# Issuing the first two gathers of a mixture-of-experts stage from the end of the routing block

## The chip, the cores and the metric

The kernel runs on one core of one Trainium2 chip. A core has five engines that run their own instruction streams and meet only through semaphores: TensorE (PE), VectorE (DVE), ScalarE (ACT), GpSimd (POOL) and SyncE (SP), which here only issues DMAs. Sixteen DMA engines carry the transfers of all of them. The metric is the device time of one execution in microseconds (us), lower being better. The kernel before takes 1161.29 us (median of three runs, 1160.04 to 1161.42).

## The reference

Two layers of a gated cross-attention network on x of 4 x 1024 tokens x 256. Layer 0 is attention over 77 context rows (16 heads), then a mixture of 8 experts with the two best experts a token; layer 1 is attention again, then a feed-forward layer with rounded weights. The change lies between the routing and the experts of layer 0:

```
x = x + tanh(g_xattn[0]) * L0_xattn(layernorm(x), ctx)
# experts of layer 0, on xt = layernorm(x), 4096 rows of 256
S = sigmoid(xt @ Wg)                    # Wg 256 x 8
G, I = top_k(S, 2)
h = gelu(einsum('nd,edf->enf', xt, W1) + b1)   # W1 8 x 256 x 1024
y = einsum('enf,efd->end', h, W2) + b2         # W2 8 x 1024 x 256
x = x + tanh(g_ffn[0]) * (sum over the two chosen experts of G * y)
x = x + tanh(g_xattn[1]) * L1_xattn(layernorm(x), ctx)
x = x + tanh(g_ffn[1]) * L1_ffn(layernorm(x))
```

## The kernel before, in words

The program is a row of blocks. At the end of each block (line 720 stands for the routing block's in the profile) every engine drains its own work and meets the others; GpSimd collects the four other engines' arrivals, then releases them, and each branches to its stream of the next block. SP's stores may still be under way at that moment: its own drain does not wait for them.

**The routing block** (`routing`, lines 697 to 1312) does two things at once. It normalises the 4096 rows, stores them to the HBM tensor `xn_dram`, forms the logits, and works out which token stands in which of 71 groups of 128 places (`C.token_of`, one column a group). It also folds the weights of the second attention ("folding"): for eight pairs of heads PE projects weights, ACT copies the products to `kst` and `vst`, and SP stores them to HBM (lines 853 and 859). The weights of the first pairs, `wkv`, arrive in a ring of two; the last pairs read `wkv_late`. The last work of each engine in this block is: PE the eighth `invert` (line 1041), DVE `tile_first` and `C.token_of` (lines 1311 and 1312), ACT the last copies to `vst` (line 1104), SP the last two stores of `vst` (line 859), GpSimd its eighth product of line 918.

**The experts block** (`experts`) works through 40 tiles: 31 of two groups (256 rows) and 9 of one. For a tile, GpSimd gathers the rows group by group with an indirect DMA (line 1491, 128 KB each) into `xg`, which has two slots; PE transposes them (line 1506, two transposes a group) to `ps_x`; ACT makes the bf16 high part `xhi` (line 1578), DVE the low part `xlo` (line 1625); PE multiplies with W1 (line 1527, 48 matmuls), ACT applies GELU (line 1590) and PE multiplies with W2 (lines 1540 and 1546). Before its first tile PE waits for the biases `b1_rows` (SP, line 1398), transposes them (line 1553), and waits for ACT's copy (line 1573); only then come the four transposes of tile 0. SP, behind `b1_rows`, waits for tile 0's two gathers (line 1455) and then loads `b2_all` (1 MB, line 1456) and the first two pieces of the next weights (line 1410).

GpSimd issues the gathers of tiles 0 and 1 one behind the other; that of tile j, from 2 on, waits until PE has transposed tile j-2. Names in the profile carry the part's prefix: `exp_xg` is `xg` of the experts, `moe_first_rows` and `all_token_of` are tensors that outlive a block.

## Time and profile before

| what | value |
|---|---|
| median of three runs | 1161.29 us (1160.04 to 1161.42) |
| the profiled execution's own time | 1163.3 us |
| its span in the trace | 1161.2 us |
| PE busy | 1057.4 us, 91% of the span |
| DVE, ACT, POOL busy | 916.9, 834.7, 539.4 us |
| share of PE in the chain that ended last | 57% |
| `L1491 POOL DMA_INDIRECT`, 71 gathers | 84.4 us busy, 1188 ns mean |
| mean granted clock of TensorE | 0.975 |

The span is what the trace covers; 2.1 us of the profiled execution lie outside it. A row of the timeline gives the start and the length in us, the engine (PEld is PE's weight load, an engine's name with q at its end is its queue, where DMAs, drains and semaphores stand), the line of the kernel, the operands, and in brackets how long the engine had been idle and what released it. The granted clock is 1.00 where TensorE has 2.4 GHz and 0.50 where it has 1.2 GHz. Most of the program is left as it is; the boundary between the two blocks lies at 336.4 us of the span.

### The profile page before, as it was taken

Reading aid. Unit: us, or ns where it says so; the run is one execution under the profiler, and the core shown is the slowest. Engines: PE = TensorE matmul, PEld = TensorE weight load, DVE = VectorE, ACT = ScalarE, POOL = GpSimd, SP = SyncE. Lnnn points to the kernel's source line nnn. Section 1 sums busy time; section 2 is a strip of 40 time slices with the busy share of each in tenths; the row PEclk is TensorE's granted clock in tenths of the full one; section 3 lists DMA queues with packets and bytes.
Section 4 is the critical chain, followed back from the end, with each engine's and each line's share of the span. In section 5 each row is a group of like instructions: output and inputs, shape, how many; then the busy total and the mean of one; then the engine's idle time right before and its main releaser. Section 6 shows DMA issues by size and latency. Waiting matters only on the chain.

```text
span 1161.2 us, 26321 instructions
## 1 busy us (share of the span) xinstructions
PE 1057.4 (91%) x8919; PEld 775.3 (67%) x8919; DVE 916.9 (79%) x1960; ACT 834.7 (72%) x2382; POOL 539.4 (46%) x515
## 2 busy tenths in 40 slices
PE   6888888868969999999999999589999999889898
PEld 5666666645537777777777777357777777645477
DVE  5999999957845687666666667479999999789798
ACT  4988889836656456556556667378888888569896
POOL 5888888732252122122122111178889887500140
PEclk9999999979989999999999999889999999989899
DMA  6443334349672343333333335345252423010034
GB/s 150 118 128 110 110 110 133 123 128 284 189 206 61 53 137 90 118 101 121 124 104 120 121 115 161 112 127 161 68 158 67 154 74 92 28 38 0 1 119 137
DMA packets 128814, 132.12 MB, mean 114 GB/s; under 512 B 24792, under 2 KB 112973, under 8 KB 128557
## 3 DMA queue, kind: packets, MB, share of 16 engines
q1 hardware_dynamic: 119901, 112.17, 32.0%
q0 software_dynamic: 6480, 17.70, 5.5%
q8 instruction: 73, 1.20, 0.4%
q10 hardware_dynamic: 2304, 0.59, 0.3%
q14 instruction: 56, 0.46, 0.1%
HBM read 82.78 MB, written 47.64 MB: 112 GB/s over the span
## 4 chain that ended last, share of the span: by engine, by line
PE 57%; DVE 4%; ACT 4%; issue 2%; DMA 1%; POOL 1%; DVEq 0%; SPq 0%; ACTq 0%; POOLq 0%
PE exp_ps_h L1527 15%; PE exp_ps_y L1540 9%; PE a_ps_o L1953 9%; PE a_ps_sc L1937 8%; PE f_ps_h L2264 5%; PE exp_ps_y L1546 5%; PE a_ps_p L1924 3%; ACT exp_h L1590 2%; DVE f_hlo L2395 2%; PE exp_ps_x L1506 1%; PE f_ps L2447 1%; PE f_ps L2443 1%; PE f_ps_x L2255 1%; DVE all_xn L2404 1%; PE a_ps_x L1911 1%
## 5 line engine op out<-in xcount | busy, mean ns | idle before, releaser
L1590 ACT ACTIVATE exp_h<-exp_ps_h,exp_b_now 128x256 f32<-128x256 f32 (+1 forms) x320 | 124.7, 440 | 142.4 <-PE exp_ps_h L1527 142.4
L1491 POOL DMA_INDIRECT exp_xg<-xn,all_token_of x71 | 84.4, 1188 | 304.0 <-PE exp_ps_x L1506 288.5
L1527 PE MATMUL exp_ps_h<-exp_xhi,exp_w_now 128*128 128x256 bf16 (+1 forms) x1280 | 196.4, 263 | 5.9 <-DVE exp_xlo L1625 5.9
L1986 ACT ACTIVATE a_z<-a_ps_sc,a_nmx 128x77 f32<-128x77 f32 x512 | 159.3, 367 | 35.6 <-DVE a_nmx L2088 35.6
L1527 PE MATMUL exp_ps_h<-exp_xlo,exp_w_now 128*128 128x256 bf16 (+1 forms) x640 | 161.4, 263 | 0.0
L1703 DVE TENSOR_TENSOR exp_hlo<-exp_h,exp_hhi 128x512 bf16<-128x512 f32 (+1 forms) x160 | 99.4, 632 | 70.4 <-ACT exp_hhi L1597 68.5
L1540 PE MATMUL exp_ps_y<-moe_w2s,exp_hhi 128*128 x568 | 134.2, 379 | 1.3 <-DVE exp_y L1722 1.3
L1527 PEld LDWEIGHTS exp_ps_h<-exp_xhi,exp_w_now 128*128 128x128 bf16 x1280 | 120.6, 99 | 20.7 <-issue 8.3
L1986 ACT ACTIVATION_READ_ACCUMULATOR a_z<-a_ps_sc,a_nmx 128x1 f32 x512 | 127.0, 248 | 0.0
L1953 PE MATMUL a_ps_o<-a_v_now,a_phi 128*128 128x256 bf16 (+1 forms) x640 | 106.6, 272 | 2.3 <-DVE a_plo L2077 2.3
L1937 PE MATMUL a_ps_sc<-a_k_now,a_xhi 128*128 128x462 bf16 (+1 forms) x384 | 98.6, 341 | 3.4 <-DMA a_k_now<-fold_klo 2.2
L1597 ACT ACTIVATE exp_hhi<-exp_h 128x512 bf16<-128x512 f32 (+1 forms) x160 | 93.1, 582 | 5.0
L1540 PEld LDWEIGHTS exp_ps_y<-moe_w2s,exp_hhi 128*128 128x128 bf16 x568 | 55.5, 98 | 52.8 <-issue 1.5
L1953 PE MATMUL a_ps_o<-a_v_now,a_plo 128*128 128x256 bf16 x320 | 87.2, 272 | 0.0
L483 PE MATMUL a_ps_vo<-a_pT,a_vblk 128*32 128x128 f32 (+1 forms) x1088 | 59.8, 279 | 27.6 <-ACT a_pT L549 20.5
L1860 POOL DMA_INDIRECT a_yg<-y_slots,all_slots x64 | 65.4, 1022 | 41.5 <-DMA y_slots<-exp_y 26.2
L379 POOL TENSOR_TENSOR a_z<-a_z,a_rsum 128x1232 f32<-128x1232 f32 x32 | 72.0, 2250 | 6.7 <-DVE a_rsum L631 6.7
L1880 POOL TENSOR_TENSOR a_z<-a_z,a_rsum 128x1232 f32<-128x1232 f32 x32 | 71.7, 2239 | 5.9 <-DVE a_rsum L2065 5.9
L1546 PE MATMUL exp_ps_y<-moe_w2s,exp_hlo 128*128 x568 | 73.6, 273 | 0.0
L1716 DVE TENSOR_TENSOR exp_yb<-exp_ps_y,exp_b_all 128x256 f32<-128x256 f32 x71 | 30.1, 424 | 54.3 <-PE exp_ps_y L1546 51.8
L1546 PEld LDWEIGHTS exp_ps_y<-moe_w2s,exp_hlo 128*128 128x128 bf16 x568 | 55.6, 98 | 21.6
L483 PEld LDWEIGHTS a_ps_vo<-a_pT,a_vblk 128*32 128x32 f32 (+1 forms) x1088 | 36.1, 109 | 50.5 <-issue 23.9
(279 smaller groups left out, 2735.5 us busy)
## 6 DMA issues: line engine op xcount, KB each, us to landing
a_stage<-in_L_ffn_W_dram SPq DMA_DIRECT2D x64, 256.0 KB, 3.2
y_slots<-exp_y SPq DMA_DIRECT2D x71, 128.0 KB, 1.7
fold_k<-route_kst SPq DMA_DIRECT2D x16, 308.0 KB, 4.5
fold_v<-route_vst SPq DMA_DIRECT2D x16, 308.0 KB
exp_job_in<-fold_k SPq DMA_DIRECT2D x14, 352.0 KB, 3.3
exp_job_in<-fold_v SPq DMA_DIRECT2D x14, 352.0 KB, 3.3
a_x<-in_x_dram SPq DMA_DIRECT2D x32, 128.0 KB, 2.3
x<-a_xo SPq DMA_DIRECT2D x32, 128.0 KB, 1.7
```

The source lines that it names most:

```text
L379: pool.tensor_tensor(zt, zt, rsum[:, v, :].unsqueeze(2).broadcast_to((P, HEADS, KEYS)), ALU.mult).then_inc(s["norm_done"], 1)
L483: mm = pe.matmul(ps_v[32 * j:32 * j + 32, g * P:(g + 1) * P], vblk[0:n, bv % 2, c, half, :], pT[0:n, c, :], start=(c == mine[0]), stop=(c ...
L1491: pool.indirect_dma_start(out=xg[:, v, u, :], out_offset=None, in_=xn_dram[:, :], in_offset=bass.IndirectOffsetOnAxis(ap=at.bitcast(U32), ...
L1527: mm = pe.matmul(hidden[:, i, f % 2, slots(j)], w1_now[:, v, k, hl, f * P:(f + 1) * P], xx[:, k, slots(j)], start=(q == 0), stop=(q == len ...
L1540: pe.matmul(ps_y[:, u, :], hhi[:, v, f, mine], w2s[:, bass.ds(e * FCH + f, 1), 0:2 * D].rearrange("p o f -> p (o f)"), start=(f == 0), sto ...
L1546: mm = pe.matmul(ps_y[:, u, 0:D], hlo[:, v, f, mine], w2s[:, bass.ds(e * FCH + f, 1), 0:D].rearrange("p o f -> p (o f)"), start=False, sto ...
L1590: ins = act.activation(h[:, f, slots(j)], hidden[:, i, f % 2, slots(j)], ACT.Gelu_apprx_tanh, bias=b1_now[:, v, f:f + 1])
L1597: act.activation(hhi[:, v, 2 * i:2 * i + 2, slots(j)], h[:, 2 * i:2 * i + 2, slots(j)], ACT.Copy).then_inc(s["hhi_done"], 1)
L1703: dve.tensor_tensor(hlo[:, v, 2 * i:2 * i + 2, slots(j)], h[:, 2 * i:2 * i + 2, slots(j)], hhi[:, v, 2 * i:2 * i + 2, slots(j)], ALU.subtr ...
L1937: mm = pe.matmul(ps_sc[:, j, 0:n], xx[:, u, k, :], k_now[:, b % 2, k, hl, h0 * KEYS:h1 * KEYS], start=(i == 0), stop=(i == len(parts) - 1))
L1953: mm = pe.matmul(ps_o[:, 0:D], pp[0:n, c, :], v_now[0:n, bv % 2, hl, c, :], start=(c == 0 and pp is phi and hl == 0), stop=last)
L1986: ins = act.activation(z[:, u, h * KEYS:(h + 1) * KEYS], ps_sc[:, j, (h - SB[j][0]) * KEYS:(h - SB[j][0] + 1) * KEYS], ACT.Exp, bias=nmx[: ...
```

## The change

GpSimd issues the two gathers of tile 0 at the end of its routing stream, after its last product. It waits there for the stored rows, for PE's last projection out of `wkv`, and for a new semaphore that DVE raises with `C.token_of`. The gathers of the experts block begin with tile 1. Their target can no longer be memory of the experts block alone: `first_rows` is allocated ahead of both blocks, with the size of `xg` (2 slots x 2 groups x 256 columns), and the folding's `wkv` is a view of it. DVE raises the new semaphore in place of its own, for which it waited once more behind `C.token_of`. SP's wait for tile 0's gathers, and its place, are unchanged.

```diff
--- before.py
+++ after.py
@@ -782,7 +782,7 @@
         ps_n = ps_x[:, 0, :].rearrange("p (a n) -> p a n", a=2)
         names = ("const_step", "wg_in", "stats_done", "mean_done", "veps_done", "rstd_done", "xn_done", "turned", "xT_done",
                  "wg_zero", "lT_done", "lT_copied", "logits_done", "filled", "emptied", "exp_done", "step", "both_done", "counted", "low_done", "high_done",
-                 "place_done", "tile_done", "inv_done", "late_in")
+                 "place_done", "tile_done", "inv_done", "late_in", "token_of_done")
         s = {n: m.sem(n) for n in names}
         xn_stored = [m.sem(f"xn_stored{i}") for i in range(2)]
         C.rows_stored, C.row_chunks = xn_stored, NCH // 2
@@ -920,6 +920,15 @@
 
             run_inversion(times_tile)
 
+            for stored_rows in C.rows_stored:
+                pool.wait_ge(stored_rows, 16 * C.row_chunks)
+            pool.wait_ge(filled, proj_at[RING_H - 1] + 3)
+            pool.wait_ge(s["token_of_done"], 1)
+            for u in range(SUB):
+                pool.indirect_dma_start(out=C.first_rows[:, 0, u, :], out_offset=None, in_=xn_dram[:, :],
+                                        in_offset=bass.IndirectOffsetOnAxis(ap=C.token_of[:, u:u + 1].bitcast(U32), axis=0)
+                                        ).then_inc(C.first_gathered[u], 16)
+
         @block.tensor
         def _(pe):
             def turn(i):
@@ -1309,7 +1318,7 @@
                     tile_experts()
             dve.wait_ge(s["inv_done"], NRI)
             link(dve.tensor_scalar(tile_first[:, :], ps_inv[:, NSUB:2 * NSUB], float(P), None, ALU.mult))
-            link(dve.tensor_tensor(C.token_of[:, :], ps_inv[:, 0:NSUB], tile_first[:, :], ALU.add))
+            dve.tensor_tensor(C.token_of[:, :], ps_inv[:, 0:NSUB], tile_first[:, :], ALU.add).then_inc(s["token_of_done"], 1)
 
 
 def experts(nc, C, xn_dram, y_dram, split, b1, b2, w_in, w_out, folded):
@@ -1342,7 +1351,7 @@
         hhi = m.sb("hhi", [P, 2, FCH, SLOT_T], BF16)
         hlo = m.sb("hlo", [P, 2, FCH, SLOT_T], BF16)
         w1_now = m.sb("w1_now", [P, 2, KD, 2, F], BF16)
-        xg = m.sb("xg", [P, 2, SUB, D])
+        xg = C.first_rows
         y = m.sb("y", [P, SUB, D])
         yb = m.sb("yb", [P, SUB, D])
         job_in = m.sb("job_in", [P, 2, WIN])
@@ -1361,7 +1370,7 @@
                  "xlo_done", "h_done", "gelu_done", "hhi_done", "hlo_done", "y_done", "y_low", "y_sum",
                  "w_turned", "job_high", "job_done", "w_step", "scale_out", "scale_in")
         s = {n: m.sem(n) for n in names}
-        gathered = [[m.sem(f"gathered{v}_{u}") for u in range(SUB)] for v in range(2)]
+        gathered = [C.first_gathered, [m.sem(f"gathered1_{u}") for u in range(SUB)]]
         stored = [m.sem(f"stored{u}") for u in range(SUB)]
         job_loaded = [m.sem(f"job_loaded{i}") for i in range(2)]
         job_stored = [m.sem(f"job_stored{i}") for i in range(2)]
@@ -1478,7 +1487,7 @@
         @block.gpsimd
         def _(pool):
             def step(j, v, n):
-                if not has(j):
+                if not has(j) or isinstance(j, int) and j == 0:
                     return
                 if has(j - 2):
                     pool.wait_ge(s["turned_x"], j - 1)
@@ -2488,15 +2497,19 @@
             w0 = {"wq": io["L0_xattn_Wq"], "bq": io["L0_xattn_bq"], "wk": io["L0_xattn_Wk"], "bk": io["L0_xattn_bk"],
                   "wv": io["L0_xattn_Wv"], "bv": io["L0_xattn_bv"], "wo": io["L0_xattn_Wo"], "bo": io["L0_xattn_bo"]}
             w1 = {"wq": io["L1_xattn_w_q"], "wkv": io["L1_xattn_w_kv"], "wo": io["L1_xattn_w_out"]}
+            C.first_rows = mm.sb("first_rows", [P, 2, SUB, D])
             with ExitStack() as front:
                 fm = Mem(nc, front, C.sems, "front")
-                ahead = {"wkv": fm.sb("wkv", [P, 2, 2, 2, P]), "wq": fm.sb("wq", [P, 2, KD, P]), "wo": fm.sb("wo", [P, 2, D]),
+                wkv_now = C.first_rows[:, :, :, :].rearrange("p v u d -> p (v u d)").rearrange(
+                    "p (g k o n) -> p g k o n", g=2, k=2, o=2)
+                ahead = {"wkv": wkv_now, "wq": fm.sb("wq", [P, 2, KD, P]), "wo": fm.sb("wo", [P, 2, D]),
                          "x": fm.sb("x", [P, AHEAD_ROWS, D])}
                 ctx_rows = ahead["x"][0:KEYS, :, :].rearrange("k r d -> k (r d)")[:, 0:B * DC].rearrange("k (b c) -> k b c", b=B)
                 with nc.Block() as C.block:
                     prologue(nc, io, C, ctx_rows)
                     attention(nc, C, x_dram, x1_dram, w0, 0, split, v_dram, ahead, w1, (io["g_xattn"], io["g_ffn"]))
                 clear_semaphores(nc, C)
+                C.first_gathered = [m.sem(f"first_gathered{u}") for u in range(SUB)]
                 routing(nc, C, x1_dram, xn_dram, io["L0_ffn_Wg"], w1, folded, ahead)
             C.block = ctx.enter_context(nc.Block())
             experts(nc, C, xn_dram, y_dram, split, io["L0_ffn_b1"], io["L0_ffn_b2"], io["L1_ffn_W_in"],
```

GpSimd's stream around the end of the routing block (line 720), as a difference; L918 is its last product, `xn` the stored rows in HBM:

```order
 L918 TENSOR_TENSOR route_high_tok<-route_high_hot,route_iota 128x8x71 x8
+L928 DMA moe_first_rows<-xn,all_token_of 128x256 x2
 L720 UNCONDITIONAL_BRANCH
-L1478 UNCONDITIONAL_BRANCH
-L1491 DMA exp_xg<-xn,all_token_of 128x256 x71
...
+L1487 UNCONDITIONAL_BRANCH
+L1500 DMA moe_first_rows<-xn,all_token_of 128x256 x69
```

Two of the 71 gathers moved in front of the branch; 69 stay behind it.

SP's stream at the same place, of the kernel before:

```order
L859 DMA fold_v<-route_vst 77x4x256 x2
L720 UNCONDITIONAL_BRANCH
L1396 UNCONDITIONAL_BRANCH
L1398 DMA exp_b_rows<-in_L_ffn_b_dram 64x128
L1456 DMA exp_b_all<-in_L_ffn_b_dram 128x2048
L1410 DMA exp_job_in<-in_L_ffn_W_in_dram 128x2x256 x3
```

And of the changed kernel:

```order
L859 DMA fold_v<-route_vst 77x4x256 x2
L720 UNCONDITIONAL_BRANCH
L1405 UNCONDITIONAL_BRANCH
L1407 DMA exp_b_rows<-in_L_ffn_b_dram 64x128
L1465 DMA exp_b_all<-in_L_ffn_b_dram 128x2048
L1419 DMA exp_job_in<-in_L_ffn_W_in_dram 128x2x256 x3
```

Nothing moved on SP but the line numbers: `b1_rows` is still issued behind the meeting of the engines, in the queue that carries the last stores of the folding.

## Rows read from the trace of the kernel before

**Rows 1.** Timeline, 318 to 350 us: start, length, engine, line, operands, idle before and releaser.

```profile
333.76 0.23 DVE L1312 TENSOR_TENSOR all_token_of<-route_ps_l,route_tile_first 128x71 int32<-128x71 f32 x1
...
335.29 0.77 SPq L859 DMA_DIRECT2D fold_v<-route_vst  x2
336.56 0.54 SPq L1398 DMA_DIRECT2D exp_b_rows<-in_L_ffn_b_dram  x1
337.41 1.23 POOL L1491 DMA_INDIRECT exp_xg<-xn,all_token_of  x1 [5.71 <-issue]
...
338.94 1.52 POOL L1491 DMA_INDIRECT exp_xg<-xn,all_token_of  x1 [0.30 <-issue]
...
339.65 0.37 PE L1553 MATMUL exp_ps_y<-all_ident,exp_b_rows 64*128 64x64 f32 x1 [6.19 <-DMA exp_b_rows<-in_L_ffn_b_dram]
340.06 0.22 ACT L1573 ACTIVATE exp_b1T<-exp_ps_y 128x64 f32<-128x64 f32 x1 [4.31 <-PE exp_ps_y L1553]
...
340.57 0.66 PE L1506 MATMUL exp_ps_x<-all_ident,exp_xg 128*128 128x128 f32 x2 [0.55 <-DMA exp_xg<-xn,all_token_of]
340.77 0.95 POOL L1491 DMA_INDIRECT exp_xg<-xn,all_token_of  x1 [0.30 <-issue]
...
342.29 0.69 PE L1506 MATMUL exp_ps_x<-all_ident,exp_xg 128*128 128x128 f32 x2 [1.07 <-DMA exp_xg<-xn,all_token_of]
...
344.42 1.23 DVE L1615 COPY exp_w_now<-moe_w1s 128x4096 bf16 x1
...
344.48 0.37 PE L1527 MATMUL exp_ps_h<-exp_xhi,exp_w_now 128*128 128x256 bf16 x1 [1.50 <-DVE exp_xlo L1625]
...
344.52 1.94 POOL L1491 DMA_INDIRECT exp_xg<-xn,all_token_of  x1 [0.30 <-issue]
```

**Rows 2.** Line 720, the end of the routing block: count, duration, start.

```profile
L720 POOLq EVENT_SEMAPHORE  x2: 17/17/17, 336.4 to 336.4; - x2
L720 POOLq DRAIN  x1: 2149/2149/2149, 329.6 to 329.6; - x1
...
L720 SPq DRAIN  x1: 7/7/7, 336.3 to 336.3; - x1
```

**Rows 3.** Line 1398, the load of b1_rows: its landing.

```profile
DMA to landing us min/median/max: 3.0/3.0/3.0
```

**Rows 4.** Line 1491, all 71 gathers: duration in ns and landing.

```profile
L1491 POOL DMA_INDIRECT exp_xg<-xn,all_token_of x71: 940/1087/1936, 337.4 to 719.0; - x71
...
DMA to landing us min/median/max: 2.7/3.2/6.3
```

**Rows 5.** Tile exp_xg, its transposes on PE: duration in ns.

```profile
L1506 PE MATMUL exp_ps_x<-all_ident,exp_xg x142: 272/273/473, 340.6 to 730.5; 128*128 128x128 f32 x142
```

**Rows 6.** DMA queues, 336 to 339 us: packets, MB, share of 16 engines.

```profile
q1 hardware_dynamic: 686, 0.65, 69.8%
```

**Rows 7.** DMA queues, 339 to 340 us.

```profile
q0 software_dynamic: 41, 0.13, 47.5%
```

**Rows 8.** Chain of work, 350 to 420 us.

```profile
354.44 7.07 PE exp_ps_h L1527 x48
...
367.58 5.24 PE exp_ps_h L1527 x48
...
384.13 0.44 PE exp_ps_x L1506 x4
```

**Rows 9.** Timeline of POOL, 340 to 420 us: a gather in the steady state.

```profile
384.84 1.36 POOL L1491 DMA_INDIRECT exp_xg<-xn,all_token_of  x1 [8.56 <-PE exp_ps_x L1506]
```

**Rows 10.** Stretches: busy us of each engine, granted clock (PEclk), DMA share, GB/s.

```profile
334.00:336.00 2.00, 0.00 (x0) 0.00 (x0) 0.00 (x0) 1.56 (x3) 0.00 (x0) 1.00 0.50 130
...
340.00:342.00 2.00, 0.68 (x3) 0.29 (x2) 0.17 (x1) 0.22 (x1) 1.42 (x2) 0.50 0.24 66
```

**Rows 11.** The same view, later stretches.

```profile
356.00:358.00 2.00, 2.00 (x11) 1.45 (x10) 1.27 (x3) 1.10 (x3) 0.00 (x0) 0.50 0.31 98
```

**Rows 12.** The same view, the steady state of the experts.

```profile
380.00:480.00 100.00, 100.00 (x777) 76.31 (x776) 75.60 (x151) 56.25 (x121) 21.38 (x18) 1.00 0.36 95
```

## The prediction

> **What bounds the kernel at this place.** I read the timeline across the boundary first, then what stands behind line 720, then the DMA queues, and last the chain of waits behind the boundary.
>
> The timeline [rows 1] shows PE idle for 6.19 us up to 339.65, and from there to 344.48 busy for a few transposes only. What it waits for changes on the way. `C.token_of`, all that a gather needs, is complete at 333.76 + 0.23 = 333.99. The engines meet at 336.4: SP's drain is the last thing before it, at 336.3, while GpSimd's drain began at 329.6, lasted 2.15 us and was over at 331.7 [rows 2]. So SP's stores hold the meeting up, and GpSimd stands idle. Behind it two paths run side by side. One is the bias: `b1_rows` is issued at 336.56, takes 3.0 us to land [rows 3], and PE transposes it at 339.65, ACT copies it at 340.06, and the first transpose of tile 0 starts at 340.57 [rows 1]. The other is the rows: the gathers are issued at 337.41 and 338.94, and the second one lets PE's second pair of transposes start at 342.29 only, 3.35 us after its issue. That pair ends at 342.98; ACT, DVE and then PE's first matmul (344.48, released by DVE's `xlo`) follow it directly. The first pair is not late by the gather to speak of: bias and gather 0 arrive together. So of all that the boundary costs, what the gathers alone cost is the time between the first pair and the second.
>
> From 354.44 on the chain lies on PE without a gap [rows 8], and PE is busy 100 of 100 us between 380 and 480 [rows 12]. What tile 0 starts earlier is therefore passed on to the end, 1:1.
>
> **The change, part by part.**
>
> *The two gathers go ahead of the meeting.* GpSimd takes 0.27 us from a release to the start of a gather: in the steady state the releasing transposes end at 384.13 + 0.44 = 384.57 [rows 8] and the gather starts at 384.84 [rows 9]. So gather 0 starts at 333.99 + 0.27 = 334.26. The issue itself costs 0.95 us where nothing disturbs it (340.77), and 1.94 where it starts beside DVE's copy of the expert weights (344.42 and 344.52) [rows 1]; the shortest and longest of 71 are 0.94 and 1.94 [rows 4]. Between 334 and 336 DVE does nothing [rows 10], so I take 0.95. The Trainium skill has the same cause (SBUF — State Buffer, SBUF: two separate sides): a DVE instruction in a two-port mode locks GpSimd out of the port through which it writes descriptors; rows 1 agree, and by the rule nothing would lock it out here. With the 0.30 us between two gathers, GpSimd is through at 334.26 + 0.95 + 0.30 + 0.95 = 336.46. At 1.94 each it would be 338.44.
>
> *The meeting.* Before, GpSimd collected the arrivals with nothing left to do. Now it arrives at 336.46, some 0.1 to 0.2 behind SP, and all engines are released about 0.15 later; at most 2.1 later with the dear gathers. Behind GpSimd's drain stands everything: it is the one that releases the others, so SP's `b1_rows`, DVE's first weight copy and its own gathers of tile 1 shift with it.
>
> *The gathers' landing.* All 71 take 2.7 to 6.3 us, 3.2 in the median [rows 4]. Gather 1 is issued at 335.51: it lands at 338.9 with 3.35, and at 341.8 with the worst. Needed is it at about 341.5 (below). So this wait goes, with a risk of 0.3.
>
> *The bias is late next.* `b1_rows` stands in SP's queue behind the two last stores of the folding, 308 KB each, issued at 335.29. That queue moves 0.65 MB between 336 and 339 and keeps the 16 DMA engines 69.8% busy, 2.09 of 3.0 us [rows 6], and no packet of a gather is among them: the first gather's 0.13 MB go by in 339 to 340, after the stores, for 47.5% of 1 us [rows 7]. Moved ahead, both gathers fall into this stretch and add 2 x 0.475 = 0.95 us: 3.04 of 3.0 us. If they fill the gaps, the bias loses nothing; if each is served in full ahead of it, 0.95. The delay of its issue by 0.15 is then hidden in the same queue. I take 0.4 for both together, near the middle, since neither end has a row nearer to it. The Trainium skill (DMA: Bandwidth & Descriptors, Queues, rings and completion order) says that a DMA engine takes turns between the queues, a packet from each; by that rule the gathers' packets are served in turn among the stores, the bias pays close to the whole 0.95, and the gain below shrinks to about 0.2. No run here shows the two mixed at this place.
>
> *Four transposes on end.* The first pair starts at 340.57 + 0.4 = 340.97. TensorE's granted clock is 0.50 here [rows 10], its lower level, after 6 us without a matmul. One transpose takes 0.473 at that level [rows 5] and the pair 0.66 to 0.69, so each further one adds 0.19 to 0.22: four take 0.47 + 3 x 0.22 = 1.13, and end at 342.10. Before: 342.98. **Gain 0.88 us.** With the ends of the bias's delay, 0 and 0.95 (and 0.15 for the meeting unhidden at the dear end), it is 1.28 to 0.18; the other side, with 2.1 of the meeting, is a rival.
>
> *Nothing else pays.* SP's wait for tile 0's gathers is over earlier, so `b2_all` and two weight pieces are issued about 3 us earlier. They come behind `b1_rows` in the same queue, and what they meet, the gathers of tile 1, is not needed before the transposes ahead of tile 1's matmuls, which start at 354.44 [rows 8], some 10 us behind. GpSimd's wait for `wkv` names a projection done long before line 918's last product. DVE's dropped wait was on its own last instruction, before the meeting: nothing. The memory is renamed and shifted, with no more or fewer transfers: nothing.
>
> Sum against the profiled execution: its span of 1161.2 becomes 1160.3, and with the 2.1 outside it 1163.3 becomes 1162.4. The median of the runs stands 2.0 below that execution; applied to it, 1161.29 - 0.88 = **1160.4 us**.
>
> **The rivals.**
>
> *A: the clock turns with the shift.* Tile 1's 48 matmuls take 7.07 us, and the same 48 of the next tile 5.24 [rows 8], because the granted clock is at its lower level again in 356 to 358 [rows 11], after PE waited in tile 0. That is 1.83 us. A tile 0 that begins earlier and more compactly could miss this stretch: 1160.4 - 1.8 = 1158.6. Against it: the wait inside tile 0, for ACT and DVE, keeps its length. The same price can fall the other way (another lower stretch is met): 1162.2.
>
> *B, the other side: the meeting waits for the data.* GpSimd's drain has had no DMA before it in this trace at line 720. If it ends only when its gathers have landed, the meeting comes at 335.51 + 3.35 + 0.1 = 338.96, 2.55 later than 336.4. By then the stores are through, `b1_rows` lands 3.0 behind its issue at 339.1 (or 2.0, an estimate: in the row the stores ahead of it ran until 339), so at 341.1 to 342.1; tile 0's transposes start 1.0 later and end 1.13 after that, at 343.2 to 344.2. That is 0.3 to 1.3 slower: up to 1162.6. It decides once the meeting is more than about 1.3 us late: 1.13 is what joining the pairs gives back. Dear gathers (1.94 each) give a meeting 2.1 late and end in the same place. [...] Against it: SP's drain took 7 ns with its stores under way [rows 2].
>
> *C: the gain is eaten whole.* The stores and gathers block each other fully, 0.95 + 0.15, and gather 1 lands at the 6.3 of the worst: nothing is left, 1161.3. The change does what it says, and another wait, the bias, has taken its place.
>
> **How the numbers follow.** Forecast 0.58; A faster 0.13, A slower 0.07; B 0.12; C 0.10. 0.2% is 2.3 us, about what a measurement here can tell from no change; the forecast, B and C lie inside it. Below 1158.97 comes only A with half a microsecond of spread between executions (the three runs differ by 1.4): 0.11. Above 1163.6 come B or A with the same spread: 0.05. The remainder is 0.84. The range reaches from 1158.4, under A, to 1162.8, over B; the forecast's own is 1159.6 to 1161.6.
>
> **What the changed profile would show.** Gather 0 starting at 334.3 us and both over by 336.5, each with 0.95; GpSimd's drain at line 720 ending there, and the semaphores behind it at 336.5 to 336.6; packets of both queues between 336 and 339; `b1_rows` landing at 339.6 to 340.5; one group of four transposes, released by ACT's `b1T` and not by a DMA; the first matmul of tile 0 at 343.4 to 344.3; SP's `b2_all` at about 339. I am wrong if the transposes still wait for a gather, if the semaphores of line 720 come behind 337.5, or if the end moves by more than the first matmul does.

## The result: a little slower, and the profile after

| | before | after |
|---|---|---|
| median of 15 runs each, us | 1161.01 (1159.96 to 1161.74) | 1163.45 (1162.40 to 1165.33) |
| ratio to before | | 1.0022, 95% interval 1.0015 to 1.0029 |
| profiled execution, its span, us | 1163.3, 1161.2 | 1163.42, 1161.5 |
| granted clock, mean | 0.975 | 0.975 |

The forecast was 1160.4, 0.6 under the median of before here. The result is 2.4 over that median and 3.1 over the forecast, outside the range, whose upper end was 1162.8. Two later comparisons of the same kernel, where the kernel before takes 1163.4 and 1163.2 us, gave 1.0011 and 1.0009, so part of the 1.0022 may belong to that first comparison and not to the kernel. The spans of the two profiled executions do not show the difference, because that of before lies over all its 15 timed runs. What they do show is where the time goes at the boundary.

The timeline of the changed kernel across the boundary (start, length, engine, line, operands, idle before and releaser):

```profile
333.87 0.23 DVE L1321 TENSOR_TENSOR all_token_of<-route_ps_l,route_tile_first 128x71 int32<-128x71 f32 x1
334.82 0.77 SPq L859 DMA_DIRECT2D fold_v<-route_vst  x2
335.03 1.23 POOL L928 DMA_INDIRECT moe_first_rows<-xn,all_token_of  x1 [3.22 <-DVE all_token_of L1321]
336.56 0.95 POOL L928 DMA_INDIRECT moe_first_rows<-xn,all_token_of  x1 [0.30 <-issue]
340.07 0.53 SPq L1407 DMA_DIRECT2D exp_b_rows<-in_L_ffn_b_dram  x1
340.71 0.53 SPq L1465 DMA_DIRECT2D exp_b_all<-in_L_ffn_b_dram  x1
340.78 1.70 POOL L1500 DMA_INDIRECT moe_first_rows<-xn,all_token_of  x1 [3.27 <-POOLq L720]
...
342.20 0.37 PE L1562 MATMUL exp_ps_y<-all_ident,exp_b_rows 64*128 64x64 f32 x1 [8.63 <-DMA exp_b_rows<-in_L_ffn_b_dram]
342.60 0.22 ACT L1582 ACTIVATE exp_b1T<-exp_ps_y 128x64 f32<-128x64 f32 x1 [7.32 <-PE exp_ps_y L1562]
...
342.88 1.12 PE L1515 MATMUL exp_ps_x<-all_ident,moe_first_rows 128*128 128x128 f32 x4 [0.31 <-ACT exp_b1T L1582]
...
345.50 0.37 PE L1536 MATMUL exp_ps_h<-exp_xhi,exp_w_now 128*128 128x256 bf16 x1 [1.50 <-DVE exp_xlo L1634]
```

Both gathers are issued ahead of the meeting, and the four transposes are one group, released by ACT and no longer by a gather, as meant. But `b1_rows`, the first thing that SP issues behind the meeting, starts at 340.07 instead of 336.56 [rows 1]. Line 720 says why:

```profile
L720 POOLq EVENT_SEMAPHORE  x2: 17/17/17, 339.9 to 340.0; - x2
...
L720 POOLq DRAIN  x1: 4600/4600/4600, 335.2 to 335.2; - x1
...
L720 SPq DRAIN  x1: 7/7/7, 335.9 to 335.9; - x1
```

SP is there at 335.9, and its drain again takes 7 ns. GpSimd's takes 4.60 us, from 335.2 to 339.8, and the semaphores that release all engines come at 339.9, where they came at 336.4 [rows 2]. Line 928, the two moved gathers:

```profile
L928 POOL DMA_INDIRECT moe_first_rows<-xn,all_token_of x2: 946/1088/1230, 335.0 to 336.6; - x2
...
DMA to landing us min/median/max: 3.1/3.1/3.1
```

The view gives a landing for gather 1 alone: it is issued at 336.56 and lands 3.1 later, at 339.66. GpSimd's drain is over 0.14 behind that. In this execution, then, it ends with the landing and not with the issue, which was through at 337.51; the experiments below test this.

The load of `b1_rows` (line 1407 now), which had taken 3.0 us [rows 3]:

```profile
DMA to landing us min/median/max: 2.1/2.1/2.1
```

It is quicker: by 340 the stores ahead of it are through, and between 340 and 341 the 16 DMA engines move nothing (share 0.00). The DMA queues between 336 and 339, to be held against [rows 6]:

```profile
q1 hardware_dynamic: 566, 0.56, 60.6%
q0 software_dynamic: 67, 0.21, 21.2%
```

The gathers' packets do share this stretch with the stores now; before, none of theirs was in it. The chain behind the boundary:

```profile
355.46 6.89 PE exp_ps_h L1536 x48
...
368.42 5.24 PE exp_ps_h L1536 x48
```

Tile 1 begins at 355.46 instead of 354.44 [rows 8], 1.02 late like the first matmul of tile 0 (345.50 instead of 344.48). Its 48 matmuls take 6.89 us instead of 7.07, and at tile 2 0.84 is left (368.42 against 367.58); at the end of the two spans it is 0.3.

**The sum, step by step.** The work ahead of the boundary shifts by up to 2 us from one execution to the next of the same kernel. I therefore count from the issue of the last two stores of the folding (line 859), which is at 335.29 before and at 334.82 after. From there:

| us | before | after | difference |
|---|---|---|---|
| to the issue of `b1_rows` | 1.27 | 5.25 | +3.98 |
| from it to PE's transposes of the bias | 3.09 | 2.13 | -0.96 |
| from these to the first transpose of the tile | 0.92 | 0.68 | -0.24 |
| from the first to the end of the fourth | 2.41 | 1.12 | -1.29 |
| from there to the first matmul | 1.50 | 1.50 | 0 |
| sum: the first matmul | 9.19 | 10.68 | +1.49 |

+1.49 of 1163 is a ratio of 1.0013.

### The profile page after: what moved, and what is told of

Its sections match the earlier page's. It is cut to its first block, busy times and chain, and to the rows that moved or that the text cites. A ratio compares the mean times of both kernels' runs of the same rounds, so it can differ in the third digit from the quotient of the medians.

```text
span 1161.5 us, 26274 instructions
## 1 busy us (share of the span) xinstructions
PE 1054.0 (91%) x8873; PEld 775.1 (67%) x8919; DVE 915.7 (79%) x1960; ACT 834.5 (72%) x2382; POOL 539.8 (46%) x515
## 4 chain that ended last, share of the span: by engine, by line
PE 57%; DVE 4%; ACT 4%; issue 2%; DMA 1%; POOL 0%; DVEq 0%; SPq 0%; ACTq 0%; POOLq 0%
PE exp_ps_h L1536 15%; PE exp_ps_y L1549 9%; PE a_ps_o L1962 9%; PE a_ps_sc L1946 8%; PE exp_ps_y L1555 5%; PE f_ps_h L2273 5%; PE a_ps_p L1933 3%; ACT exp_h L1599 2%; DVE f_hlo L2404 2%; PE exp_ps_x L1515 1%; PE f_ps L2456 1%; PE f_ps L2452 1%; PE f_ps_x L2264 1%; ACT a_z L1995 1%; DVE all_xn L2413 1%
## 5 line engine op out<-in xcount | busy, mean ns | idle before, releaser
L1500 POOL DMA_INDIRECT moe_first_rows<-xn,all_token_of x69 | 82.3, 1192 | 301.1 <-PE exp_ps_x L1515 288.7
L1549 PE MATMUL exp_ps_y<-moe_w2s,exp_hhi 128*128 x529 | 125.8, 379 | 3.4 <-DVE exp_y L1731 1.3
```

Source lines behind the costliest of these rows:

```text
L1500: pool.indirect_dma_start(out=xg[:, v, u, :], out_offset=None, in_=xn_dram[:, :], in_offset=bass.IndirectOffsetOnAxis(ap=at.bitcast(U32), ...
L1549: pe.matmul(ps_y[:, u, :], hhi[:, v, f, mine], w2s[:, bass.ds(e * FCH + f, 1), 0:2 * D].rearrange("p o f -> p (o f)"), start=(f == 0), sto ...
```

## The experiments

My theory after the result (theory D in what follows) was rival B of the prediction: GpSimd's drain waits for the landing, holds every engine at the meeting, and what the joined transposes give back is less than that. The rivals were the memory, which the change also rearranges; the block's end itself; the clock (rival A); and the DMA queues, where the gathers now meet the stores. Every kernel below was timed against the kernel before on the same chip. The one number by which I compare them is the start of tile 0's first matmul, counted from the stores' issue. The four executions of the first row, with tile 0's gathers, the bias and the meeting where they were, give 9.19, 9.28, 9.23 and 9.28, 9.25 in the mean. That is the zero of the column "by it". All columns but the last two are us behind the stores; the meeting is the later of GpSimd's two semaphores of line 720, whose time the view gives to a tenth. The last column is the measured ratio with its 95% interval. Of each kernel's runs one was profiled, and these columns are read from it.

| kernel | meeting | bias on PE | first matmul | by it the ratio is | measured |
|---|---|---|---|---|---|
| before, `e1_before_again`, `e3_memory_only`, `e4_before_no_drain` | 1.11 to 1.22 | 4.36 to 4.39 | 9.19 to 9.28 | 1 | 0.9991, 0.9995, 0.9999 |
| after | 5.18 | 7.38 | 10.68 | 1.0012 | 1.0022 [1.0015, 1.0029] |
| `a1_after_again` | 5.36 | 7.55 | 10.86 | 1.0014 | 1.0011 [1.0001, 1.0021] |
| `c4_after_third` | 5.22 | 7.41 | 10.70 | 1.0012 | 1.0009 [1.0000, 1.0018] |
| `e2_no_drain` | 1.28 | 6.38 | 9.68 | 1.0004 | 0.9997 [0.9988, 1.0005] |
| `a2_bias_early` | 5.26 | 5.45 | 8.72 | 0.9995 | 0.9994 [0.9983, 1.0004] |
| `a3_bias_early_no_drain` | 1.28 | 1.40 | 7.24 | 0.9983 | 0.9979 [0.9970, 0.9988] |
| `c1_both_again` | 1.23 | 1.40 | 7.18 | 0.9982 | 0.9985 [0.9974, 0.9997] |
| `c2_bias_early_only` | 1.12 | 1.32 | 9.20 | 1.0000 | 0.9994 [0.9984, 1.0004] |
| `a4_held` | 2.54 | 5.84 | 10.65 | 1.0012 | 1.0008 [0.9998, 1.0018] |
| `c3_one_gather` | 2.06 | 4.48 | 7.88 | 0.9988 | 1.0003 [0.9991, 1.0014] |

The expectations of the second and third round still count from the end of `C.token_of`. By that the four executions of the first row spread over 10.5 to 11.3, and the changed kernel's three over 11.4 to 12.9; by the stores it is 0.09 and 0.18. I chose the stores as the start after seeing this.

**First: before again, the drain taken away, the memory alone.** The kernel before, unchanged, measures what "no change" looks like. No edit.

> The kernel before, unchanged, under another name. All theories: ratio 1.000 within 0.0007, near 1161.0 us. It gives a second profile of the kernel before, because the first one (1163.3 us) lay 2.3 above the median of its runs (1161.01). If TensorE's clock explains that, this profile has no stretch at the lower level between 354 and 359 us, and tile 1's 48 matmuls take about 5.3 us in it instead of 7.07; if it does not, the two profiles differ by less than 0.5 us up to 370.

Measured: 1163.10 us, 0.9991 [0.9981, 1.0001]. The same kernel against itself comes out nearly 0.1% off, so an interval that just misses 1 is no finding. Its timeline:

```profile
336.93 0.77 SPq L859 DMA_DIRECT2D fold_v<-route_vst  x2
338.20 0.53 SPq L1398 DMA_DIRECT2D exp_b_rows<-in_L_ffn_b_dram  x1
...
341.29 0.36 PE L1553 MATMUL exp_ps_y<-all_ident,exp_b_rows 64*128 64x64 f32 x1 [6.90 <-DMA exp_b_rows<-in_L_ffn_b_dram]
...
342.20 0.66 PE L1506 MATMUL exp_ps_x<-all_ident,exp_xg 128*128 128x128 f32 x2 [0.55 <-DMA exp_xg<-xn,all_token_of]
...
344.02 0.69 PE L1506 MATMUL exp_ps_x<-all_ident,exp_xg 128*128 128x128 f32 x2 [1.17 <-DMA exp_xg<-xn,all_token_of]
```

Everything is 1.6 us later than in [rows 1], by the clock of the span, and within 0.1 the same counted from the stores: the bias is on PE 4.36 behind them in both. This is what made me count from there. Neither sign that I had named came: tile 1's 48 matmuls took 7.03 and not 5.3, and yet the two profiles lie more than 0.5 apart.

The changed kernel without GpSimd's drain at the end of the routing block:

```
-        block = ctx.enter_context(nc.Block())
+        block = ctx.enter_context(nc.Block(no_gpsimd_drain=True))
```

> The changed kernel, whose routing block ends with a meeting that leaves out GpSimd's drain. Theory D (the drain waits until the gathers' data have landed, 4.6 us, and that holds all engines up): the meeting moves from 340.0 to about 337.6, when the second gather's issue is over; b1_rows is issued at 337.7, tile 0's first matmul starts near 343.6 instead of 345.5, and the time falls from 1163.4 to 1160.0 to 1161.0. Theory L (the loss comes from the new memory or from gathers that share the DMA engines with the stores): stays at 1163.0 to 1163.7, though the meeting is earlier.

Measured: 1163.22 us, 0.9997 [0.9988, 1.0005]. Its timeline, and then the landing of `b1_rows`:

```profile
335.91 1.23 POOL L928 DMA_INDIRECT moe_first_rows<-xn,all_token_of  x1 [3.22 <-DVE all_token_of L1321]
336.42 0.77 SPq L859 DMA_DIRECT2D fold_v<-route_vst  x2
337.45 0.95 POOL L928 DMA_INDIRECT moe_first_rows<-xn,all_token_of  x1 [0.30 <-issue]
337.79 0.54 SPq L1407 DMA_DIRECT2D exp_b_rows<-in_L_ffn_b_dram  x1
...
342.80 0.37 PE L1562 MATMUL exp_ps_y<-all_ident,exp_b_rows 64*128 64x64 f32 x1 [8.34 <-DMA exp_b_rows<-in_L_ffn_b_dram]
...
343.48 1.12 PE L1515 MATMUL exp_ps_x<-all_ident,moe_first_rows 128*128 128x128 f32 x4 [0.31 <-ACT exp_b1T L1582]
```

```profile
DMA to landing us min/median/max: 5.0/5.0/5.0
```

Without the drain the meeting is back at 1.28 behind the stores, and SP issues `b1_rows` at 337.79, 1.37 behind them, although gather 1 is not issued before 337.45. So it is the drain that held the meeting, and by 3.9 us. Without it GpSimd does not even stay for its own issue: the semaphores come at 337.6 to 337.7, and gather 1 is being issued until 338.40. But of the second half of my expectation only part comes: the first matmul is at 9.68 and not at 8.8 (343.6 less 334.82), and the kernel is no faster than before. That is what theory L had named, gathers that share the DMA engines with the stores. `b1_rows` now takes 5.0 us, 3.0 in [rows 3]: it stands behind the stores, and the gathers go by beside these. They are more than tile 0's two: with the meeting early, tile 1's first gather is issued at 338.70, and by 342 the gathers' queue has moved 0.37 MB, where two gathers are 0.26. What each adds is not parted here. In place of the 0.4 us of the prediction it is 2.0, more than the 1.3 that joining the transposes gives. The Trainium skill (DMA: Bandwidth & Descriptors, Queues, rings and completion order) says that a DMA engine takes turns among the queues. This run agrees in kind, with 0.14 MB of gathers and 0.51 MB of SP's queue moved between 336 and 340; in size it costs more than the 0.95 us that I had worked out for two gathers from [rows 7].

The changed kernel's memory with the gathers where they were: `first_rows` and its semaphores stay, line 928's block goes.

```
-            for stored_rows in C.rows_stored:
-                pool.wait_ge(stored_rows, 16 * C.row_chunks)
...
-            for u in range(SUB):
-                pool.indirect_dma_start(out=C.first_rows[:, 0, u, :], ...
...
-                if not has(j) or isinstance(j, int) and j == 0:
+                if not has(j):
```

> The changed kernel's memory (first_rows ahead of both blocks, the folding's wkv as a view of it), with all 71 gathers back in the experts block. Theory D: as the kernel before, 1160.6 to 1161.5 us, meeting at 336.4. Theory L, memory: 1162.5 to 1163.5 us.

Measured: 1163.53 us, 0.9995 [0.9984, 1.0006], and the first matmul at 9.23, within the 9.19 to 9.28 of the others. No cost of the memory is to be seen, and by the interval it is under 0.7 us.

The kernel before with the same form of block end as in `e2_no_drain`, the same one-line edit:

> The kernel before with the meeting at the end of the routing block without GpSimd's drain, as in e2. It is the control for the other form of meeting. Theory D: GpSimd's drain was over at 331.7, long before the last engine, so nothing changes: 1160.6 to 1161.5 us. If the form of the meeting is itself worth something, it shows here and is to be taken off the gain of e2.

Measured: 1163.38 us, 0.9999 [0.9989, 1.0010], first matmul at 9.28. Where GpSimd has nothing under way, its drain costs nothing, since SP's stores are what is last there.

**Second: the bias taken from behind the stores.** If the bias is what the rest waits for, its load must stand somewhere else. Here SP issues it in the routing block, at 287 us of the span, into memory that a piece of the folding's weights had. With this go a few moves of memory (`yb`, `xhi`, `xlo`, `b1_now`), and ACT's wait for the folding's stores comes a little earlier in its stream. `c2_bias_early_only` below shows that all this alone changes nothing.

```
+            sp.wait_ge(filled, proj_at[2] + 3)
+            sp.dma_start(C.b1_rows[:, :], C.b1.rearrange("e (c f) -> (e c) f", f=P)).then_inc(C.bias_in, 16)
...
-            sp.dma_start(b1_rows[:, :], b1.rearrange("e (c f) -> (e c) f", f=P)).then_inc(s["bias_in"], 16)
...
-        yb = m.sb("yb", [P, SUB, D])
+        yb = C.wq_now.rearrange("p a k n -> p a (k n)")
```

With it went the changed kernel, unchanged, on the same chip:

> The changed kernel, unchanged, beside the other three on one chip. The first measurement gave a ratio of 1.0022 [1.0015, 1.0029]; its profile shows the start of tile 0 only about 1 us later than the kernel before. Theory D (the drain holds the meeting 3.6 us, of which joining the transposes and an unburdened DMA queue give back 2.6): 1.0003 to 1.0015. Theory M (more than the boundary changed, the rest is lost further on): 1.0022 again, with spans that differ by more than the boundary does.

Measured: 1164.38 us, 1.0011 [1.0001, 1.0021]; the drain took 5.31 us, with a landing of 3.9 for gather 1.

> The changed kernel, and SP loads b1_rows in the routing block already, into memory that the folding's wq has left; GpSimd's drain is kept. Theory D: the drain still ends with the gathers' landing, the meeting stays 5.9 us behind C.token_of, but PE starts with the bias right behind it: first matmul of tile 0 about 2.0 us earlier than in the changed kernel, ratio to the kernel before 0.9985 to 0.9997. Rival (the bias was not what was late behind the meeting): as the changed kernel.

Measured: 1162.95 us, 0.9994 [0.9983, 1.0004]. The PE rows of its timeline:

```profile
342.09 0.34 PE L1564 MATMUL exp_ps_y<-all_ident,moe_wq_now 64*128 64x64 f32 x1 [7.83 <-PEq L720]
...
342.74 1.12 PE L1517 MATMUL exp_ps_x<-all_ident,moe_first_rows 128*128 128x128 f32 x4 [0.31 <-ACT exp_b1T L1584]
```

PE's first work behind the boundary is released by the meeting itself (`PEq L720`), the bias being there long before. The bias no longer costs a landing behind the meeting, and the first matmul is 1.96 earlier than in the changed kernel, as expected. What is left is the drain: 5.88 us in this execution.

Both edits together:

> As a2, and the meeting leaves out GpSimd's drain. Theory D: both waits are gone, the transposes wait for the gathers' landing alone (5.5 us behind C.token_of, second gather), the first matmul comes 2.5 to 3.5 us earlier than in the kernel before: ratio 0.9970 to 0.9982. If the gathers land later because the stores share the DMA engines, 0.9982 to 0.9992.

Measured: 1161.05 us, 0.9979 [0.9970, 0.9988]. Its timeline:

```profile
337.62 0.77 SPq L859 DMA_DIRECT2D fold_v<-route_vst  x2
338.06 0.95 POOL L930 DMA_INDIRECT moe_first_rows<-xn,all_token_of  x1 [0.30 <-issue]
...
339.80 0.66 PE L1517 MATMUL exp_ps_x<-all_ident,moe_first_rows 128*128 128x128 f32 x2 [0.53 <-DMA moe_first_rows<-xn,all_token_of]
...
342.67 0.69 PE L1517 MATMUL exp_ps_x<-all_ident,moe_first_rows 128*128 128x128 f32 x2 [2.21 <-DMA moe_first_rows<-xn,all_token_of]
...
344.86 0.37 PE L1538 MATMUL exp_ps_h<-exp_xhi,exp_w_now 128*128 128x256 bf16 x1 [1.50 <-DVE exp_xlo L1636]
```

The first matmul comes 7.24 behind the stores, 2.0 earlier than before. The transposes are two pairs again, the second released by gather 1, which was issued at 338.06 and releases PE only at 342.67. So the gathers, too, are slow beside the stores (4.6 us), but they are now the only thing that is waited for. The ratio lies in the range that I gave for theory D, the first matmul does not: 2.0 earlier than before and not 2.5 to 3.5, which is the expectation's other case, gathers that land late. The same kernel again:

> The kernel of a3 once more (gathers and bias ahead of the meeting, no drain of GpSimd in it), to see whether its gain holds beside another set of runs: ratio 0.9970 to 0.9988, 0.9979 before. Theory D and no rival: it is the version that should beat both kernels.

Measured: 1161.20 us, 0.9985 [0.9974, 0.9997], with the first matmul at 7.18. This version beats the kernel before by 0.21 and 0.15% in two comparisons, and the changed kernel on the same chip by 3.3 and 3.2 us (1164.38 and 1164.41 less these).

The kernel before with its meeting held by something else: GpSimd repeats line 918's product three times behind `C.token_of`.

```
+            pool.wait_ge(s["token_of_done"], 1)
...
+            for turn in range(3):
+                wait(pool, s["held"], turn)
+                pool.tensor_tensor(high_tok[:, 0, :, :, 1, :], high_hot[:, 0, :, :, :], again, ALU.mult).then_inc(s["held"], 1)
+            pool.wait_ge(s["held"], 3)
```

> The kernel before, and GpSimd repeats its product of line 918 three times behind C.token_of (some 6.4 us of ordinary work, no DMA, the same values again), so that the meeting comes about 4.3 us later than it did. This measures what a late meeting alone costs. If it is passed on 1:1: 4.0 us more, ratio 1.0033 to 1.0040. If part of it is given back because b1_rows then finds its queue empty (it landed 2.1 us behind its issue in the changed kernel, 3.0 in the kernel before): 3.1 us, ratio 1.0025 to 1.0030.

Measured: 1164.72 us, 1.0008 [0.9998, 1.0018]. The hold in its timeline, beside the stores and the first gather:

```profile
334.10 3.56 POOL L927 TENSOR_TENSOR route_high_tok<-route_high_hot,route_iota 128x568 bf16<-128x568 bf16 x3 [2.38 <-DVE all_token_of L1320]
...
335.46 0.77 SPq L859 DMA_DIRECT2D fold_v<-route_vst  x2
...
338.96 1.83 POOL L1499 DMA_INDIRECT exp_xg<-xn,all_token_of  x1 [1.31 <-issue]
```

And its line 720:

```profile
L720 POOLq DRAIN  x1: 34/34/34, 337.8 to 337.8; - x1
```

The three products took 3.56 us and not the 6.4 that I had expected from their cost in the folding, so the meeting is only 1.36 later than the usual 1.18. The first matmul is 1.40 later. The size missed, and with it the expected ratio; what this one execution shows is that the late meeting goes on to the first matmul in full. (Gather 1 starts 2.0 later, since gather 0's issue takes 1.83, but lands 0.5 to 0.6 sooner.) In the changed kernel 3.98 are late and 2.49 are given back. The drain is the other finding: behind 3.56 us of products that are over, and with no gather under way, it takes 34 ns. So it has no fixed price of several us.

**Third: which part of the gain is whose.** The early bias without early gathers, against `a2_bias_early`:

```
-            for u in range(SUB):
-                pool.indirect_dma_start(out=C.first_rows[:, 0, u, :], ...
...
-                if not has(j) or isinstance(j, int) and j == 0:
+                if not has(j):
```

> The changed kernel's memory and the early b1_rows, with all 71 gathers behind the meeting as in the kernel before. It tells what of a3 is the bias alone. Theory D: behind the meeting the second gather is what PE waits for last, so the bias alone gives nothing: first matmul 10.5 to 11.3 us behind C.token_of, ratio 0.9995 to 1.0005. Rival (the bias is all there is to gain, the gathers add nothing): ratio as a3, 0.9979 to 0.9988.

Measured: 1162.42 us, 0.9994 [0.9984, 1.0004]; first matmul at 9.20. The transposes of its tile 0:

```profile
340.18 0.66 PE L1509 MATMUL exp_ps_x<-all_ident,moe_first_rows 128*128 128x128 f32 x2 [3.74 <-DMA moe_first_rows<-xn,all_token_of]
...
341.89 0.69 PE L1509 MATMUL exp_ps_x<-all_ident,moe_first_rows 128*128 128x128 f32 x2 [1.04 <-DMA moe_first_rows<-xn,all_token_of]
```

The first matmul is 11.1 behind `C.token_of`, as expected; the ratio lies 0.0001 under the expected range. PE now waits for the gathers, both times. The early bias alone gives nothing, and the early gathers alone give nothing, even without the drain (`e2_no_drain`). Together they give 0.5 in the first matmul with the drain (`a2_bias_early`), which the ratio cannot tell from no change, and 2.0 without it.

Gather 0 alone ahead of the meeting:

```
-            for u in range(SUB):
+            for u in range(1):
...
-                if not has(j) or isinstance(j, int) and j == 0:
+                if not has(j):
...
-                for u in subs(j):
+                for u in subs(j)[1 if isinstance(j, int) and j == 0 else 0:]:
```

> The changed kernel with only the first of tile 0's gathers ahead of the meeting, the drain kept. Theory D: the drain ends with that gather's landing, 4.1 to 5.5 us behind C.token_of (5.9 and 6.6 with both), and the second gather comes behind it as in the kernel before, so tile 0's first matmul is the latest of all, 12.3 to 13.3 us behind C.token_of; ratio 1.0011 to 1.0025. Rival (the drain costs a fixed 4.6 us or more whatever is under way): the meeting stays at 5.9 to 6.6 us and the first matmul comes at 13.5 or later, ratio over 1.0025.

Measured: 1164.22 us, 1.0003 [0.9991, 1.0014]. Line 720, and then its timeline:

```profile
L720 POOLq EVENT_SEMAPHORE  x2: 17/17/17, 338.1 to 338.2; - x2
...
L720 POOLq DRAIN  x1: 3459/3459/3459, 334.6 to 334.6; - x1
```

```profile
334.89 1.23 POOL L928 DMA_INDIRECT moe_first_rows<-xn,all_token_of  x1 [3.22 <-DVE all_token_of L1321]
...
339.04 0.94 POOL L1500 DMA_INDIRECT moe_first_rows<-xn,all_token_of  x1 [2.92 <-POOLq L720]
...
341.30 1.22 PE L1515 MATMUL exp_ps_x<-all_ident,moe_first_rows 128*128 128x128 f32 x4 [0.31 <-ACT exp_b1T L1582]
```

The drain is shorter, 3.46 us, and ends at 338.1, as expected 4.1 behind `C.token_of` and 3.2 behind the issue of the one gather ahead of it. The meeting is 2.06 behind the stores, still 0.9 later than without early gathers. The first matmul comes at 7.88, 1.37 earlier than before, and that makes 0.9988. Here my expectation missed: counted from `C.token_of` it is 10.05 and not 12.3 to 13.3, since gather 1, issued at 339.04, lands at 341.8, while PE is still at the first two transposes, and the four stay one group. The kernel was measured at 1.0003, and the low end of its interval just misses that. The runs fell into two groups, four of 1160.15 to 1162.18 and seven of 1163.85 to 1165.68, and the profiled one was the fastest of all, 1160.15. What parts the two groups no trace shows, since only one was profiled. So whether half of the change is a gain stays open.

And the changed kernel a third time:

> The changed kernel a third time. It was 1.0022 [1.0015, 1.0029] at first and 1.0011 [1.0001, 1.0021] on a chip whose runs lie further apart. From the start of tile 0 in the profiles (11.4 and 12.1 us behind C.token_of, against 10.5 to 11.3 in four of the kernel before's kind) follows 1.0006; what the runs show beyond that has another cause. Expected 1.0005 to 1.0020.

Measured: 1164.41 us, 1.0009 [1.0000, 1.0018]. Line 928, then line 720:

```profile
L928 POOL DMA_INDIRECT moe_first_rows<-xn,all_token_of x2: 946/1088/1230, 335.6 to 337.2; - x2
...
DMA to landing us min/median/max: 4.7/4.7/4.7
```

```profile
L720 POOLq DRAIN  x1: 6127/6127/6127, 335.8 to 335.8; - x1
```

Here gather 1 lands at 337.16 + 4.7 = 341.86, and the drain ends at 335.8 + 6.13 = 341.93. In every execution that has the drain and both early gathers the two agree:

| | gather 1 lands | drain ends | drain, us |
|---|---|---|---|
| after | 339.66 | 339.8 | 4.60 |
| `a1_after_again` | 340.8 | 340.8 | 5.31 |
| `a2_bias_early` | 341.7 | 341.8 | 5.88 |
| `c4_after_third` | 341.86 | 341.93 | 6.13 |

The landing ranged over 1.6 us, from 3.1 to 4.7, and the drain's end went with it. By the semaphores' own times in the trace, which the views round to a tenth, the drain ends 0.13 us behind gather 1's last increment in all four, and in `c3_one_gather` 0.09 behind gather 0's.

When gather 1 lands does not follow from when it is issued. In the six executions with both gathers early, other than `e2_no_drain`, its issue starts 0.1 to 1.7 behind the stores, and it lands (in `a3_bias_early_no_drain`: releases PE) 4.8 to 5.1 behind them; in `e2_no_drain` 5.9. It looks as if the stores set this time. No run moved the stores to test it. With the drain this landing is what places the meeting, at 5.2 to 5.4 in all four rows.

## Why the prediction was wrong

**The bound and the chain: right as far as shown.** PE waited for the bias and then for gather 1. That the end follows the first matmul 1:1 is borne out in the main: of thirteen measured ratios eleven have what the first matmul alone gives inside their interval; the first timing of after and `c3_one_gather` have it just outside. It is no sharp test, since nine of the intervals also hold 1. In single profiles it can't be seen: from the first matmul to the end of the span it is 814.1 to 816.7 us in the fourteen executions, and 816.0, 815.5 and 814.8 in the changed kernel's three.

**The step that failed: "The meeting".** I let GpSimd arrive when its gathers were issued, at 336.46, and the engines meet at about 336.6. They met at 339.9, and so the bias, the next thing waited for, was issued 3.98 later, counted from the stores. GpSimd's drain ends with the landing of gather 1, as the table above shows, and without it (`e2_no_drain`) the meeting is back where it was. Rival B said exactly this, with a chance of 0.12. Its argument against was SP's drain of 7 ns with stores under way; SP's still takes 7 ns, so that row was read rightly, but it says nothing of GpSimd's. The only row of GpSimd's own drain, 2.15 us [rows 2], had no DMA before it, but it could have warned me: it lay over the engine's last product (2.05 us from 329.65), so this drain already was a wait for work under way, and with none it takes 34 ns (`a4_held`). An unknown that no row bounds deserved much more than 0.12, the more so as its price, 0.3 to 1.3, was worked out and it would turn the sign.

**B's size: 1.5 instead of 0.3 to 1.3.** Its form held (meeting late, bias lands 2.1 behind its issue, four transposes on end). The meeting was later than its 338.96 by 0.9 on the clock of the span; counted from the stores it was 5.2 to 5.4 instead of 3.67. The term that failed is the landing of 3.35 behind the issue: in `c4_after_third` gather 1 was issued 0.28 behind the stores, almost where I had put it (335.51 is 0.22 behind), and still landed at 4.98 behind them, 4.7 after its issue. That the stores would slow the gathers I had counted with only in rival C. GpSimd's start was short by 0.94 as well: gather 0 starts 0.93 behind the end of `C.token_of`, not 0.27 as in the steady state, and its issue takes 1.23, not 0.95, in all eight executions with early gathers. Both could be read in [rows 1], where the first gather behind the meeting of 336.4 starts at 337.41 and takes 1.23. Nor is 1.13 "what joining the pairs gives back": it is how long four transposes take. Joining gives 2.41 - 1.13 = 1.28 (measured 1.29), and with the quicker landing of the bias (0.96) and a first transpose that no longer waits for gather 0 (0.24) 2.49 came back: by these sizes a meeting 2.5 late would have been paid back, and this one was 4.0 late.

**"The bias is late next": right in kind, wrong by five times.** I took 0.4, between 0 and 0.95. In the changed kernel this cannot be seen, since the late meeting has moved the bias out of the stores' way. `e2_no_drain` shows it: 5.0 against 3.0, so 2.0, of which tile 1's first gather, which I had called harmless, may have a part. Had the drain not waited, the forecast of a gain would have failed still: 0.4 late in the first matmul (9.68 against 9.25) instead of 0.88 early, though a difference that small is not told from none (0.9997 [0.9988, 1.0005]). These are two failing steps, of which either alone would have taken the gain.

**"Four transposes on end": right.** 1.13 expected, 1.12 measured. Released by ACT's `b1T`, as expected.

**"Nothing else pays": right as far as the runs tell.** Memory and the dropped wait show no cost (`e3_memory_only`). SP's `b2_all` came at 340.71 rather than 339, with the meeting.

**Rival A, the clock: not shown.** The stretch at the lower level falls differently from one execution to the next: tile 1's 48 matmuls took 7.07, 7.03, 7.07 and 7.07 us in the four executions of the table's first row, 6.89 in after, and 5.40 in the nine others. Among these nine are two whose gathers stand behind the meeting as before (`a4_held`, `c2_bias_early_only`), and the two further executions of the changed kernel, so early gathers do not decide it. Eight of the nine were taken on a chip on which the kernel before was not profiled, so whether the kernel or the chip decides it stays open. The chain of `a1_after_again`:

```profile
356.45 5.40 PE exp_ps_h L1536 x48
...
367.92 5.24 PE exp_ps_h L1536 x48
```

It gains 1.49 us on after in this tile, and yet from the first matmul to the end of the span it is only 0.5 shorter (815.5 against 816.0); other stretches take the rest back. One profile of each says too little on this. The first timing of after gave 1.0022 where the first matmul gives 1.0012, 1.2 us more, of which 0.3 lie outside its interval; that may be the clock or the chip, and stays open.

## What to carry to other kernels

Work that is issued ahead of a block's end is not done ahead of it: look for what the end itself waits for, engine by engine, and where no row shows that engine's drain with transfers under way, give both readings a real chance. If the wait that is removed stands beside another of about its length (here the bias and gather 1, 1.3 us apart), move both or neither: each alone gave nothing or worse, both gave 0.15 to 0.21% once the drain was gone too. (Half of the change, one gather early, stays an open case.) And look at what large stores and new transfers do to each other both ways: here the small load behind the stores came 2.0 us later, and the gathers beside them 1.2 to 1.7 later than the median.

## What the hardware did that I had not expected

- GpSimd's drain at the end of a block waits for the data of its gathers, 3.46 us with one and 4.60 to 6.13 with two, and ends about 0.1 us behind the landing; with no gather under way it took 34 ns. SP's takes 7 ns with its stores under way.
- `b1_rows`, 64 rows of 128 floats, lands in 2.0 to 2.1 us with the stores through, in 3.0 to 3.1 when issued 1.3 us behind them, and 5.0 behind the stores with three gathers issued beside them.
- The gathers suffer as well beside the stores: gather 1 took 4.4 to 4.9 us to land in five executions, 3.9 and 3.1 in the two others, where the median of all gathers in [rows 4] is 3.2. But for `e2_no_drain`, the later it was issued behind the stores, the less it took.
- GpSimd's first gather behind its products started 0.93 us after its release and took 1.23 to issue, the second 0.95, with VectorE idle.
- Three of line 918's products on end, with VectorE idle, took 3.56 us, 1.19 each, where one in the folding, beside other work, takes 2.05.
